# Two attention layers and a mixture of experts on one core: expert weights loaded later, one b2 product per expert bank, batch 0's results listed behind batch 1's chain

## The reference, cut to what matters

```
x = LN(x + attn0(x))                        # 8 heads of 16, causal, a rank-one term added to the scores
r = rmsnorm(x)                              # latent attention: 16 heads of 8, rotary, causal
x = x + mla(r, Wq, Wdkv, Wuk, Wuv, Wo)
h = relu(rmsnorm(x) @ W1[e].T + b1[e])      # e = 0..3, 512 hidden units each
y = h @ W2[e].T + b2[e]
x = LN(x + y of the expert with the largest gate)
```

## Time and profile before

| | |
|---|---|
| median of 3 runs | 638.15 us (635.68 to 639.89) |
| the profiled execution, its own time | 640.52 us |
| its span, first to last instruction | 637.5 us |
| mean granted TensorE clock | 0.958 of 2.4 GHz |
| TensorE busy | 564.9 us (89%) |
| VectorE busy | 418.5 us (66%) |
| ScalarE busy | 346.3 us (54%) |
| GpSimd busy | 157.9 us (25%) |

### The profile page before, as it was taken

One profiled execution on the slowest core, in us unless ns is written; L12 is line 12 of the kernel. 1 busy time (PEld: TensorE's weight loads), 2 busy tenths in 40 slices (PEclk: granted clock), 3 DMA queues, 4 the chain that ended last, 5 costly groups with the idle time before them and its releaser, 6 DMA issues.

```text
span 637.5 us, 10797 instructions
## 1 busy us (share of the span) xinstructions
PE 564.9 (89%) x3917; PEld 264.1 (41%) x3933; DVE 418.5 (66%) x1063; ACT 346.3 (54%) x673; POOL 157.9 (25%) x217
## 2 busy tenths in 40 slices
PE   6668499879799988989999999999999998899993
PEld 3323133443343333333333335445444453256662
DVE  4489388877876878887888777756776614214403
ACT  4313266647456667656777776555556556643230
POOL 9620121325343126543030213101102102101000
PEclk9769699989899999989999999999999999899998
DMA  4956303001021002011010001001000000000000
GB/s 129 203 146 225 93 2 99 2 27 46 5 67 41 21 3 75 26 52 51 19 34 28 26 22 32 1 3 51 15 5 2 1 3 18 0 1 2 17 0 17
DMA packets 27846, 25.64 MB, mean 40 GB/s; under 512 B 7377, under 2 KB 24401, under 8 KB 27538
## 3 DMA queue, kind: packets, MB, share of 16 engines
q1 hardware_dynamic: 27410, 24.17, 13.5%
q0 software_dynamic: 384, 0.79, 0.6%
HBM read 17.30 MB, written 7.34 MB: 39 GB/s over the span
## 4 chain that ended last, share of the span: by engine, by line
PE 65%; DVE 9%; ACT 9%; SPq 7%; issue 4%; DMA 3%; POOL 2%; another core or an unknown queue 0%; DVEq 0%; ACTq 0%; POOLq 0%
PE ps L1201 14%; PE ps L1277 11%; PE ps L1184 10%; PE ps L1333 10%; PE ps L1163 7%; ACT pr L1353 6%; SPq L892 4%; PE ps L1266 3%; DVE mparts L1575 3%; PE ps L1260 2%; PE ps L1212 2%; PE ps L1275 2%; PE ps L1241 2%; PE ps L1158 1%; DMA scr0k<-parts 1%
## 5 line engine op out<-in xcount | busy, mean ns | idle before, releaser
L1353 ACT ACTIVATE pr<-ps 128x512 f32<-128x512 f32 (+1 forms) x480 | 248.4, 555 | 187.1 <-PE ps L1184 154.8
L1575 DVE TENSOR_REDUCE mparts<-ps 128x1 f32<-128x512 f32 (+3 forms) x480 | 277.5, 629 | 89.1 <-PE ps L1163 87.8
L1163 PE MATMUL ps<-ks,qs 61*128 61x512 bf16 (+7 forms) x576 | 147.9, 341 | 18.9 <-DMA qs<-nparts 9.3
L1184 PE MATMUL ps<-qs,ks 64*128 64x512 bf16 (+7 forms) x560 | 141.0, 331 | 14.4 <-ACT pr L1353 9.3
L1201 PE MATMUL ps<-pr,vs 128*32 128x512 f32 (+3 forms) x1152 | 123.6, 501 | 5.7 <-ACT pr L1353 3.1
L1057 POOL TENSOR_SCALAR_AFFINE_SELECT pr<-pr 128x512 f32<-128x512 f32 x96 | 61.5, 640 | 270.3 <-ACT pr L1353 270.0
L1184 PEld LDWEIGHTS ps<-qs,ks 64*128 64x128 bf16 (+1 forms) x576 | 42.4, 95 | 129.8 <-ACT pr L1353 86.2
L1277 PE MATMUL ps<-w,work 128*128 128x128 f32 x512 | 74.1, 288 | 0.0
L1333 PE MATMUL ps<-feat,w 128*128 128x512 f32 x128 | 67.9, 636 | 0.1
L1163 PEld LDWEIGHTS ps<-ks,qs 61*128 61x128 bf16 (+1 forms) x576 | 49.0, 98 | 44.7 <-DVE mparts L1575 27.1
L1429 ACT ACTIVATE work<-ps,b 128x512 f32<-128x512 f32 x64 | 43.9, 687 | 38.9 <-PE ps L1333 38.3
(11 more groups left out here) (138 smaller groups left out, 500.0 us busy)
## 6 DMA issues: line engine op xcount, KB each, us to landing
qs<-scr0q SPq DMA_DIRECT2D x48, 64.0 KB, 4.4
qs<-scr1q SPq DMA_DIRECT2D x84, 32.0 KB
ks<-scr1k SPq DMA_DIRECT2D x84, 32.0 KB
ks<-scr0k SPq DMA_DIRECT2D x36, 64.0 KB, 2.2
scr0q<-parts SPq DMA_DIRECT2D x4, 384.0 KB, 3.2
scr0k<-parts SPq DMA_DIRECT2D x4, 384.0 KB, 4.9
scr1q<-parts SPq DMA_DIRECT2D x4, 384.0 KB, 2.5
scr1k<-parts SPq DMA_DIRECT2D x4, 384.0 KB, 2.6
```

Of the source, the lines that this page charges most:

```text
L1163: last = pe.matmul(bank[:, h, :], queries(F, 0, h0 + h, i * P, P), keys(F, 0, h0 + h, 512 * c, w), start=not diagonal, stop=True, skip_gro ...
L1184: last = pe.matmul(to[:, h, :], keys(F, 3, h0 + h, j * P, P), queries(F, 3, h0 + h, qb * 512 + lo, n), start=True, stop=True)
L1353: act.activation(pr[:, st % PSLOTS, h0:h0 + nh, 0:STEPS[st][3]], scores_at(F, v), ACT.Exp, scale=GROUPS[F][0].scale).then_inc(exped, 1)
L1575: dve.tensor_reduce(mparts[:, F % SLOTS, h0:h0 + nh, i, c], maxes_at(F, u), AX_X, ALU.max).then_inc(taken, 1)
```

## The change

It has three parts, and the list of steps is built anew from them.

1. **Expert weights later.** W1, W2 and b1 become a step of their own, `moe_weights`, at position 1.5 and behind `rows` (2, 2). `weights` keeps 15 DMAs and now needs `rows` (0, 1) instead of `rows` (0, 0). `b2_parts` moves from position 0.6 to 1.1 and behind `rows` (1, 2), `partners` from 0.7 to 1.05. The idle time that a step would cause on SP counts five times, and the costs say that weights, stores and the GpSimd load land later.
2. **One product opens a bank.** Instead of one b2 product of 128 columns ahead of each quarter, the first quarter's step issues one product over the whole bank of 512 columns, with the b2 row read four times by a step of zero. The three other quarters add to it.
3. **Results listed later.** The result steps of a block leave `experts` and get positions of their own, 13.5 to 14.2, behind the chain that prepares batch 1's experts.

```diff
@@ experts / results
-    return out + [("moments", 2, b, i)] + root("result", b, (i,)) + [("layer_norm", 2, b, i), ("out", b, i)]
+    return out
+def results(b, i):
+    return [("moments", 2, b, i), *root("result", b, (i,)), ("layer_norm", 2, b, i), ("out", b, i)]
@@ wanted
             add("result", spread(experts(b, i), *EXPERTS[b][i]))
+            add("result", spread(results(b, i), *RESULTS[b][i]))
-    add("once", [(0.05, ("weights",)), (0.6, ("b2_parts",)), (0.7, ("partners",)), (1.2, ("halves",)),
+    add("once", [(0.05, ("weights",)), (1.1, ("b2_parts",)), (1.05, ("partners",)), (1.2, ("halves",)), (1.5, ("moe_weights",)),
+RESULTS = [[(13.5, 13.6), (13.6, 13.7)], [(14.0, 14.1), (14.1, 14.2)]]
@@ costs
+SP_IDLE = 5.0
-         "hat": (POOL, 1.3), "x12": (POOL, 1.3), "gate": (PE, 0.95), "pick": (DVE, 2.1), "hidden": (PE, 0.9),
-         "relu": (ACTE, 0.6), "expert": (PE, 1.27), "pick_up": (DVE, 1.4), "layer_norm": (DVE, 1.4), "out": (SP, 0.5),
-         "copy_v": (POOL, 0.66), "pads": (POOL, 3.6), "ones": (POOL, 4.0), "halves": (POOL, 1.7), "weights": (SP, 9.5),
+         "hat": (POOL, 1.3), "x12": (POOL, 1.3), "gate": (PE, 0.95), "pick": (DVE, 2.1), "hidden": (PE, 1.0),
+         "relu": (ACTE, 0.6), "expert": (PE, 1.15), "pick_up": (DVE, 1.4), "layer_norm": (DVE, 1.4), "out": (SP, 0.5),
+         "copy_v": (POOL, 0.66), "pads": (POOL, 3.6), "ones": (POOL, 4.0), "halves": (POOL, 1.7), "weights": (SP, 5.2), "moe_weights": (SP, 1.1),
+    if kind == "expert" and step[4] == 0:
+        return [(PE, 1.45)]
-X_READY = [5.0, 6.0, 7.0, 8.0]
+X_READY = [4.5, 6.3, 7.0, 8.0]
+LANDS_LATER = {"weights": 4.0, "moe_weights": 10.0, "store": 1.0}
+POOL_LANDS = 4.0
@@ needs
     if kind == "hidden":
-        return [("feat", "hat1", *a[:2]), ("lo", 15), ("v_proj", 1, 1, 1), ("weights",)]
+        return [("feat", "hat1", *a[:2]), ("lo", 15), ("v_proj", 1, 1, 1), ("moe_weights",)]
     if kind == "b2_parts":
-        return [("weights",), ("store", 5)]
+        return [("weights",), ("store", 5), ("rows", 1, 2)]
     if kind == "weights":
-        return [("rows", 0, 0)]
+        return [("rows", 0, 1)]
+    if kind == "moe_weights":
+        return [("rows", 2, 2)]
@@ order
-        return at - max(issued, 0 if first == PE else free[first]), at
+        idle = at - max(issued, 0 if first == PE else free[first])
+        return (SP_IDLE if first == SP else 1) * idle, at
@@ block.sync
+            def moe_weights():
                 for dst, src in [(w1[:, :], "W1T"), (w2[:, :, :], "W2T"), (b1[:, :], "b1T")]:
                     sp.dma_start(dst, a[src]).then_inc(moe_in, 16)
@@ expert
-                pe.matmul(to, ones3[0:3, :], b2p[0:3, e * C:(e + 1) * C], start=True, stop=False, skip_group_check=True)
+                if t == 0:
+                    pe.matmul(side("expert", b, i, e, 0).rearrange("p (t c) -> p t c", c=C), ones3[0:3, :],
+                              b2p[0:3, e * C:(e + 1) * C].unsqueeze(1).broadcast_to([PARTS, 4, C]),
+                              start=True, stop=False, skip_group_check=True)
```

More of the change, by code:

```diff
@@ L613, in order @@
         end[step] = time
-        if kind == "weights":
-            end[step] += 6.0
+        if kind in LANDS_LATER:
+            end[step] += LANDS_LATER[kind]
+        if step[:3] == ("load", 0, 1):
+            end[step] += POOL_LANDS
         if kind in ("max", "turn", "turnmax"):
@@ L772, in build @@
         done = {k: sem("done_" + k) for k in STEP_KINDS if k not in (
-            "scores", "max", "store", "load", "rows", "out", "quiet", "weights", "turn", "turnmax",
+            "scores", "max", "store", "load", "rows", "out", "quiet", "weights", "moe_weights", "turn", "turnmax",
             "b2_parts", "combine")}
@@ L960, in _ @@
                     weights()
+                elif kind == "moe_weights":
+                    moe_weights()
                 elif kind == "b2_parts":
```

2 lines of the change are left out of this document (1 added, 1 removed).

## The result

The changed kernel takes 618.86 us (median of 4 runs, 613.35 to 619.56) against 637.61 (4 runs) of the kernel before: a ratio of 0.9686, 95% interval 0.9621 to 0.975, so 2.5 to 3.8% faster. Run again later on another occasion it took 616.75 us (6 runs) against 639.22: 0.9676 (0.9639 to 0.9712). The forecast was 626.0 us with a range of 620.0 to 634.5. The front came about as forecast; the price of the b2 product and what a rebuilt list is worth were not.

The account below looks back on a forecast made before the run. TensorE was taken to bound from 374 us, TensorE and VectorE in turns from 96, waits before. Front -6.5, product -5.1, results -0.5 sum to -12.1: 638.15 to 626.0 us, range 620 to 634.5.

Parts of the forecast that it names:

- The front: First 96 us: rows (0, 1) ahead of the weights brings VectorE to its old stop earlier, -6.5 us (-2.5 to -8.5).
- the wait at the first score: Front: first scores wait for rows (0, 0), landing at 48.3, and VectorE starves until 49.0: +2.6 us.
- the second half's first reductions: Front: maxima of the second half cannot start before 35.36; the later load of keys (1, 0) adds 0.5 us.
- The 15th reduction behind `combine`: Front: VectorE does at 69.1 us what it did at 75.65, which gives the -6.5 us.
- all later moves of the front are nothing: Front: moved load of group 2, partners, b2_parts and moe_weights cost nothing; up to 3 us in the upper bound.
- the clock not falling: Front: condition, together with no crowding or front cost, for the bound of 2 us more gain, -8.5.
- The product: Experts: 64 narrow b2 products become 16 wide ones, -5.1 us (-4.0 to -5.9).
- the third term: Result steps of batch 0 listed later: VectorE work mostly hidden, so -0.5 us (0 to -1).
- Of 1.24 us per quarter the b2 product takes 0.15: Experts: each narrow b2 product costs 0.15 us to the next start, so 64 of them 9.6 us.
- The wide product's price: Experts: a 512-column b2 product takes 0.26 us, between 0.23 and 0.31; 16 of them 4.2 us.
- Columns count: Rival, 10%: b2 product time grows with columns, 16 wide products cost 0.6 us each, 9.6 in all; 631.2 us.
- The rival with three chains behind the last product: Rival, 3%: result chains do not fit between the pick_ups and follow TensorE's last product, costing 15.6 us; 641.6 us.

Follow-up runs that it names:

- second execution: The changed kernel profiled once more, without an edit, against its first profiled execution: span 613.9 us beside 611.6; median of its runs 616.75 us.

## Why the prediction was too small

**The front: forecast -6.5 (bounds -2.5 to -8.5), measured -8.7 to -9.1, just beyond its bound.** The chain of steps was right. `combine` (0, 1) was forecast at 59.9 and came at 60.01 in the second execution (56.48 in the first). Its terms were off in ways that cancel: the wait at the first score was 1.0 to 1.3 us, not 2.6, and the second half's first reductions came at 38.2 instead of 36.5. The 15th reduction behind `combine`, which stood at 75.65 before, starts at 63.37 + 11 x 0.56 = 69.5, where the step said 69.1. What failed is the sentence behind it, that all later moves of the front are nothing. By `rows` (3) the executions in the new order are 8.2 us ahead on average (185.0 against 193.3, eight and five executions), by `rows` (8) 8.7. (`rows` (1) is 9.7 us earlier in the second execution, 86.80 against 96.47, since VectorE now splits b2, 2.6 us of work, behind it and no longer ahead of it.) About 2 us more than the 6.1 at that place come after it. Short waits of VectorE, which before sum to 0.43 + 0.42 + 0.67 + 0.48 + 0.27 = 2.3 us from 76 us to `rows` (1) and in the second execution to 0.37 + 0.46 + 0.23 = 1.1, are one part. Another may be the clock, which the forecast took up only as a bound ("the clock not falling"). In before the granted clock is 0.50 from 68.2 to 78.2 us, from within the stop to behind it. From the end of the stop to `rows` (3) TensorE is busy for 103.7 us at 0.95 (75.65 to 193.25), and for 102.6 us with as many products (674 against 675) at 0.97 in the second execution (69.53 to 184.81). No run holds the clock still, so the clock's share stays open.

The forecast took the moves of `partners` and `b2_parts` for free. They cost nothing; but without them two thirds of the gain would have gone. The list of the queue's readers was not read for who now waits for late weights, and it came out right only because the change had seen to it. That the weights of the experts are split off, which gives the change its name, is worth nothing that the times show.

**The product: forecast -5.1 (bounds -4.0 to -5.9), measured -9.1 to -10.6 by the ratios, -8.8 to -10.4 by the traces.** This is the step that failed by most. Its excess over its own bound, 2.9 to 4.7 us, is more than the 1.1 us by which the median left the range; the excess of the third term would have been enough too. "Of 1.24 us per quarter the b2 product takes 0.15" reads the product by its place in the queue and leaves the quarter's 1.09 us as they are. But in a row 0.2 of these are there only because a b2 product stands on either side, so that such a product costs 0.35. The trace of before showed both halves. One is at the last quarter of the same expert:

```profile
593.75 0.23 PE L1275 MATMUL ps<-b2p,ones 3*128 3x128 bf16 x1
593.90 1.16 PE L1277 MATMUL ps<-w,work 128*128 128x128 f32 x8
594.90 1.45 PE L1333 MATMUL ps<-feat,w 128*128 128x512 f32 x3
```

The four f32 products with a b2 product ahead and an f32 product behind take 1.00 us, those with one on both sides 1.09. That alone opens the upper bound from 0.15 to 0.24 us per product, 64 x 0.09 = 5.8 us more. The other half shows only in single records: in every quarter of before the first one takes 0.21 us to the next start and the ones behind it 0.11. The wide product's price, 0.26 with 0.31 as the upper bound, was 0.31 to 0.32. "Columns count" was wrong (0.6 us forecast). The Trainium skill, "TensorE: Matmul & The Clock Gate", in the steps of an issued matmul, has throughput as purely the number of columns. By that the change of 64 x 128 to 16 x 512 columns is worth nothing, and the four narrow products in a row, 0.32 us like the wide one, agree with it. It does not hold where the kind of product changes: there 128 columns of bf16 cost 0.15 to 0.35 us.

**The results: forecast -0.5 (0 to -1), measured -2.7 to -4.8.** The reasoning, that the chain lies beside other work, was right for the chain itself: moved by hand it is worth 0.5 us, with an interval from -1.0 to 2.0. What failed is that the term priced only the steps named. The list is built anew, and TensorE's idle time from `rows` (8) on falls from 6.7 to 3.8 us. That a chain of 5.2 us fits into the idle time ahead of the last `pick_up` held: 0.88 us are left of it. The rival with three chains behind the last product did not come.

**The sum.** -8.9, -9.7 and -3.7 (the middles of the measured) are -22.3, against -20.0 by the ratio of the first comparison and -20.7 (-18.4 to -23.1) by that of the second. Forecast was -12.1 with all three terms small to the same side. The range was built with the three bounds and 2 us for the spread of the runs, and all three terms ended beyond their bounds for a gain.

## What to carry to other kernels

Read a small product's cost from the distance between the products around it with and without it, not from its own place: a bf16 product between f32 products costs its place and lengthens one f32 record ahead of it and one behind. When a transfer is moved back in a queue, move every reader of it back on its own engine in the same step, or the wait only changes the engine. And where a planner builds the list, a part that touches its lanes is worth what the new list is worth: price it as unknown, even if the steps it moves are hidden. Here it was 3 to 5 us faster. When TensorE waits more often, look at the granted clock as well as at the waits: with the quarters grouped, 12.5 us more of waiting came with 8.2 us more of busy time.

## What the runs showed of the hardware

- Four f32 products of 128 columns take 0.89 us between f32 products, whatever line these come from, 0.99 with a bf16 product on one side and 1.09 with one on both, by the starts in the timelines. A change between bf16 and f32 costs 0.1 us in either direction. Four bf16 products of 128 columns in a row take the same 0.32 us as one of 512.
- A product with the start flag on one quarter of a PSUM bank seems to open the whole bank. The kernel with four narrow products in a row, each with the flag, deviates from the reference by 0.0383, the one without b2 by 0.0442; the ratio is 0.866, the root of 3/4, as if b2 were lost in three quarters of four. In the kernel before, a quarter is complete when the next flag comes, so nothing is lost. This was argued from the two numbers and not looked at further.
- The same program's `rows` (0, 1) lay 3.5 us apart in two executions (59.92 and 63.46). 2.1 us of that were there by `rows` (0, 0), behind the first loads; the rest arose up to `rows` (0, 1), while the granted clock was 0.50 instead of 1.00 (45.0 to 54.1 us). 2.2 us were left at `rows` (8).
